# A fused convolution, attention and expert kernel: other fillers, a shorter group deviation, reordered output products

## The chip, the core and the metric

The kernel runs on one core of a Trainium2 chip. The metric is device time in microseconds (us), from one launch; several runs are made and their median is taken. The core has five engines that run side by side and meet at semaphores: TensorE (matrix products, into PSUM), VectorE, ScalarE, GpSimd and SyncE (which here issues the transfers).

## The reference

The input x has 4 images of 64 channels of 16 x 16 pixels. Three layers follow, each added to its input:

```python
x = x + involution(group_norm(x))          # 32 groups of 2 channels
t = tokens(x)                              # 4 x 256 tokens of 64
t = t + attention(layer_norm(t))           # 8 heads
t = t + experts(layer_norm(t))             # 8 experts, 2 used by an image
```

- group_norm: mean and variance over 2 channels and all pixels, `(g - m) / sqrt(s + eps)`.
- involution: from x a 1x1 convolution to 16 channels, batch norm with given statistics, relu, and a 1x1 convolution to 49 weights for each of 4 groups; each pixel is the sum of its 7 x 7 neighbours with these weights; then a 1x1 projection.
- attention: for each head, q^T k over all tokens gives a 64 x 64 matrix, which is normalised by its own mean and variance, put through a softmax, and applied to v; then the output projection Wo.
- experts: the mean over an image's tokens gives logits, a softmax, a scaling by expected load, a second softmax, and the two best experts; each is a gelu layer of 128 and a linear layer back, mixed by the gates; then a layer norm with gamma and beta.

## The kernel before

The program is written out engine by engine; every engine runs its own list in order, and waits for semaphores. Two images lie side by side in the 128 partitions (64 channels each), so there are two pairs of images, `t_` = 0 and 1, and four blocks of 128 tokens (`NQ` = 4). Nothing loops at run time.

Results of TensorE go to 8 PSUM banks. `CHUNKS` lists the results in the order in which they are made, with the engine that reads each; `SHARED` says which takes over the bank of another, and `homes` places the rest round the banks. `begin(name)` on TensorE waits until the earlier holder of the bank was read (`wait_read`), and returns the bank. An fp32 product takes two passes on TensorE, each a weight load and a matmul.

`keep_warm(name, n, cols)` issues `n` products of a tile of zeros, `cols` columns wide, whose results nobody uses; it calls `begin` first, also where `n` is 0. `WARM` holds the counts. "Filler" means such a product below.

The stages that matter here, in their order:

- Start. TensorE runs seven fillers, then one behind the arrival of `xg`, one behind the channel moments, one behind the root of the variance ("group_deviations"), and then the group product (`gn0`, `gn1`), which adds up the two channels of a group and spreads mean and scale. Its factors `gs` are made on VectorE (L675 to L685): the inverse deviation from ScalarE's root, and one correction step on it. The batch-norm scale is made in the same way in between, in `bn_t`. Then VectorE normalises (`normalise`, L697), TensorE multiplies with w1 (`y`), ScalarE applies scale, shift and relu (L530), and three "spread" products and the window transposes (L1003) follow.
- The involution's products, then the projection and the layer norm of tokens; the gram matrix of the tokens (`gram_part`, four of them, with fillers between), from it the heads' scores (`a..`), the row products (`rows`: 32 passes on `gm` and `wqc`), four transposes of `e` (L1154), and the variance of the scores from the row squares and the sums of squares `ast`.
- The softmax, then the value products `v00` to `v11`, read by VectorE as `pv` (L820 for the first half of the heads, L825 for the second), and the output products of pv and the centred Wo (`woc`), which add up in `m`: the heads in four steps `i`, in each the two partition halves `l` and the two pairs `t_`.
- `m` is copied to SBUF by VectorE and ScalarE; four products of `eT` and `m` add to the residual products in `o0` to `o3`; squares, roots and scales give `f`, which TensorE sums and transposes (`fsum`, `fT`, L1220) behind six fillers. `b2_products` is a small product, used much later; `restore` keeps o plus beta for the end, eight steps, of which the last stands late.
- Logits, softmax, choice (`pick`), which VectorE and GpSimd load into registers to copy the chosen weights (L342); the expert products; the squares of the result (`nq`), their roots, and the output.

## Time and profile before

| | |
|---|---|
| median of 3 runs | 54.08 us (53.98 to 54.11) |
| the profiled execution | 53.69 us |
| its span in the profile | 51.8 us |
| TensorE matmul busy | 42.9 us (83% of the span) |
| VectorE, ScalarE, GpSimd busy | 35.2, 31.6, 16.4 us |

The profile is one execution. Its span starts with the first instruction and ends with the last; some 1.9 us of the device time lie outside. Matmuls are pipelined, and their ends are modelled: two that overlap both count, so the starts say more than the busy time. All times in rows are us from the start of the span, durations in us unless marked ns.

### The profile page before, as it was taken

To read this page: it belongs to the slowest core of one execution; us is meant where nothing else is said; L and a number is where in the kernel's file an instruction comes from. 1 tells how busy PE (TensorE), PEld (TensorE's weight loads), DVE (VectorE), ACT (ScalarE), POOL (GpSimd) and SP (SyncE) were. 2 spreads that over 40 slices of the span, in tenths; PEclk is the share of its full clock that TensorE was granted. 3 is DMA by queue.
4 is the path that set the end of the run, shared out by engine and by line. 5 is a ranking of instruction groups with operands and counts; after the bars stand their busy time and mean duration, and the time that the engine had idled before them with its cause. 6 is when DMAs were issued, how large, how long until landed. Compare 5 with 4: busy or idle time off the path is not lost.

```text
span 51.8 us, 1844 instructions
## 1 busy us (share of the span) xinstructions
PE 42.9 (83%) x678; PEld 30.2 (58%) x678; DVE 35.2 (68%) x143; ACT 31.6 (61%) x92; POOL 16.4 (32%) x45
## 2 busy tenths in 40 slices
PE   0999989999998989799499588799976899999400
PEld 0331343799996966489367467584831367869300
DVE  3788996567997986460909269459968387983940
ACT  0363419969856794265339992279965967996200
POOL 5996009100038730983000000630000279332000
PEclk9999999999999999999999999999999999999985
DMA  0499888465000000000000006600000000000051
GB/s 0 129 326 286 218 234 223 114 89 173 8 0 13 0 0 0 6 13 0 0 6 0 0 13 133 272 0 0 13 0 0 0 0 0 6 0 0 0 150 53
DMA packets 3608, 3.21 MB, mean 62 GB/s; under 512 B 912, under 2 KB 2960, under 8 KB 3600
## 3 DMA queue, kind: packets, MB, share of 16 engines
q1 hardware_dynamic: 3072, 2.80, 19.5%
q10 hardware_dynamic: 432, 0.30, 2.0%
q8 instruction: 5, 0.08, 0.6%
q0 software_dynamic: 96, 0.00, 0.2%
q14 instruction: 3, 0.02, 0.1%
HBM read 2.84 MB, written 0.26 MB: 60 GB/s over the span
## 4 chain that ended last, share of the span: by engine, by line
PE 66%; DVE 13%; issue 7%; ACT 6%; DVEq 1%; ACTq 0%
PE ps L968 61%; PE ps L1003 3%; DVE res L955 3%; ACT L585 2%; DVE pv L825 1%; DVE pv L820 1%; PE ps L1220 1%; ACT prob L588 1%; PE ps L1154 1%; ACT yf L530 1%; DVE xp L697 1%; DVEq L335 1%; ACT rt L608 1%; DVE rsum L817 1%; DVE m L833 1%
## 5 line engine op out<-in xcount | busy, mean ns | idle before, releaser
L968 PE MATMUL ps<-zeros 128*128 128x512 bf16 (+1 forms) x38 | 11.6, 426 | 1.7 <-DVE zeros L664 1.2
L968 PEld LDWEIGHTS ps<-zeros 128*128 128x128 bf16 x38 | 3.4, 107 | 6.1 <-issue 1.4
L622 ACT ACTIVATE h<-ps,b1s 128x256 f32<-128x256 f32 x8 | 3.2, 473 | 0.8 <-PE ps L968 0.8
L319 DVE COPY wt<-ps 128x512 f32<-128x512 f32 x4 | 2.7, 688 | 1.3 <-PE ps L968 1.2
L342 POOL COPY w1s_g<-fw 128x128 f32 x4 | 1.2, 292 | 7.3 <-DVE pick L904 6.8
L968 PEld LDWEIGHTS ps<-yc,taps 128*128 128x128 bf16 x128 | 3.3, 96 | 0.3 <-issue 0.3
L968 PE MATMUL ps<-yc,taps 128*128 128x32 bf16 x128 | 3.4, 176 | 0.1
L450 POOL TENSOR_SCALAR w2m<-w2m 128x8 f32<-128x8 f32 x1 | 0.2, 245 | 9.0 <-DVE w2m L830 9.0
L482 ACT ACTIVATE wt<-ps 128x512 f32<-128x512 f32 x4 | 2.3, 596 | 0.7 <-PE ps L968 0.6
L479 ACT ACT_TABLE_LOAD x1 | 1.3, 1283 | 2.1 <-issue 2.1
L968 PE MATMUL ps<-fT,w1s 64*128 64x256 f32 x8 | 2.3, 403 | 0.2 <-DVE w1s L342 0.2
L1003 PE MATMUL ps<-consts,xp 128*128 128x128 f32 x16 | 2.4, 282 | 0.0
L482 ACT ACTIVATE xw<-ps 128x512 f32<-128x512 f32 x4 | 2.3, 592 | 0.0
L968 PE MATMUL ps<-fT,w1s_g 64*128 64x256 f32 x8 | 2.2, 398 | 0.0
L968 PE MATMUL ps<-wt,xw 128*32 128x64 f32 x128 | 2.2, 220 | 0.0
L368 POOL COPY taps<-w2c 128x140 bf16<-128x140 bf16 (+1 forms) x3 | 1.2, 493 | 3.1 <-DVE w2c L709 3.1
L805 DVE TENSOR_REDUCE ast<-asq 128x8 f32<-128x512 f32 x2 | 1.3, 680 | 1.2 <-ACT asq L576 1.2
L423 POOL TENSOR_SCALAR wkm<-wks 128x8 f32<-128x8 f32 x1 | 0.2, 243 | 5.7 <-DVE wks L732 5.7
L968 PE MATMUL ps<-h,w2s 128*64 128x256 f32 x16 | 2.1, 386 | 0.0
L968 PEld LDWEIGHTS ps<-wt,xw 128*32 128x32 f32 x128 | 1.9, 110 | 0.2
L407 POOL MEMSET taps<- 128x2240 bf16 x1 | 2.0, 1967 | 0.0
L864 DVE SCALAR_TENSOR_TENSOR t2b<-ps,betas 128x64 f32<-128x64 f32 x8 | 1.9, 274 | 0.0
(202 smaller groups left out, 120.0 us busy)
## 6 DMA issues: line engine op xcount, KB each, us to landing
fw<-in_fw SPq DMA_DIRECT2D x1, 512.0 KB, 3.6
wvT<-in_wvT SPq DMA_DIRECT2D x1, 260.0 KB, 3.6
x<-in_x SPq DMA_DIRECT2D x2, 128.0 KB, 3.9
wq<-in_L_attn_Wq SPq DMA_DIRECT2D x2, 128.0 KB, 3.1
wk<-in_L_attn_Wk SPq DMA_DIRECT2D x2, 128.0 KB, 3.4
fw<-in_fw SPq DMA_DIRECT2D x1, 256.0 KB, 3.8
out<-res SPq DMA_DIRECT2D x4, 64.0 KB, 1.6
xg<-in_x ACTq DMA_DIRECT2D x1, 128.0 KB, 2.8
```

The source lines that it names most:

```text
L319: copy(wt[:, :, :, :, :, g, w0:w0 + 8].rearrange("p l t q r w -> p (l t q) r w"), src.rearrange("p (w r q) -> p q r w", w=8, r=2)).then_in ...
L342: eng.tensor_copy(dst[:, b // 2, k, :].unsqueeze(1), fw1[:, bass.ds(expert, 1), :]).then_inc(copied, 1)
L368: copy(dst, w2c[:, :, :, lo:hi]).then_inc(done, 1)
L407: return pool.memset(ap, 0.0).then_inc(const[name], 1)
L479: act.preload_act_table(ACT.Sqrt)
L482: return act.activation(dst, src, ACT.Copy)
L622: act.activation(h[:, b, k, :], bank(f"h{TOPK * t_ + k}{l}")[:, 0:HW], ACT.Gelu, bias=b1s[:, b, k:k + 1]).then_inc(read_a, 1)
L805: dve.reduce_sum(ast[:, i, :, :], asq[:, i, :, :, :], AX.X).then_inc(made["score_sums"], 1)
L864: ins = dve.scalar_tensor_tensor(t2b[:, j, :], tokens(f"o{i}")[:, l, :], bank(f"o{i}")[:, l * (TC - 1):l * (TC - 1) + 1], betas[:, l, :], ...
L955: ins = dve.scalar_tensor_tensor(res[:, j, :], bank(f"u{i}")[:, (j - 2 * i) * C:(j - 2 * i + 1) * C], nrs[:, j:j + 1], t2b[:, j, :], ALU.m ...
L968: return pe.matmul(dst, lhsT, rhs, start=start, stop=stop)
L1003: ins = pe.transpose(dst[:, j * P:(j + 1) * P], xp[:, t_, 2 * q:2 * q + WINR, :], ident)
```

## The change

- Start: twelve short fillers (64 columns, 32 rows of the result) are put in after the seven long ones, ahead of the wait for `xg`. VectorE makes the reciprocal of the variance while ScalarE takes the root, and the scale is then root times that reciprocal plus the reciprocal of the root, in one step, without the correction (the signs and the factor in the `group` matrix change with it). The batch-norm scale is made in the same form, and two steps of ScalarE change places.
- The single fillers of 512 columns around the gram parts become four of 128 columns; one filler more behind the logits and one more behind the loads.
- `pv` of the first half of the heads is made in two steps, as that of the second half. The output products wait for each step, alternate between the halves `l` inside the pairs `t_`, and have no `keep_warm` of zero fillers between. `m` takes the bank that `o3` had, and `o3` that of `v00`; the residual product of `o3` moves behind the products of `m`.
- `b2_products` moves behind the four products with `m`, its read on VectorE behind the last normalisation.
- The last `restore` moves ahead of the register loads of the choice.
- Half of the second pair's squares is made on VectorE.

```diff
-WARM = {"start": 7, "stats": 2, "bands": 1, "norm1": 1, "gram": 1, "last": 4, "scores": 2, 
-        "values": 0, "m": 2, "output": 6, "norm2": 0,
-        "logits": 2, "choice": 3, "loads": 4}
+WARM = {"start": 7, "short": 12, "stats": 2, "norm1": 4, "last": 4, "gram": 4, "scores": 2,
+        "output": 6, "logits": 3, "choice": 3, "loads": 5}
...
-    ("o1", "O"), ("o2", "O"), ("o3", "O"), ("m", "V"),
+    ("o1", "O"), ("o2", "O"), ("m", "V"), ("o3", "O"),
...
-SHARED = {"gm0": "d3", "gm1": "gram", "m": "v00", "fsum": "v00", ...
+SHARED = {"gm0": "d3", "gm1": "gram", "o3": "v00", "fsum": "m", ...
...
+            act.wait_ge(dma["w2"], 16)
+            copy(w2a[:, :], w2r[:, :]).then_inc(made["w2_first"], 1)
             act.wait_ge(dma["front"], 16)
             act.activation(bn_t[:, 0:1], bnv[:, 3:4], ACT.Sqrt, bias=eps[:, :]).then_inc(made["bn_std"], 1)
-            act.wait_ge(dma["w2"], 16)
-            copy(w2a[:, :], w2r[:, :]).then_inc(made["w2_first"], 1)
...
-            act.activation(nq[:, 1, :], sums[:, 1, :], ACT.Square).then_inc(made["squared_by_scalar"], 1)
+            act.activation(nq[:, 1, TOK:], sums[:, 1, TOK:], ACT.Square).then_inc(made["squared_by_scalar"], 1)
...
-            dve.tensor_scalar(gs[:, 0:1], gmv[:, 0:1], -2.0, None, ALU.mult).then_inc(made["group_scales"], 1)
+            dve.tensor_scalar(gs[:, 0:1], gmv[:, 0:1], 2.0, None, ALU.mult).then_inc(made["group_scales"], 1)
+            after_mark()
+            mark(dve.reciprocal(gd[:, 3:4], gd[:, 1:2]))
             dve.wait_ge(dma["front"], 16)
             mark(dve.tensor_scalar(bn_t[:, 1:2], bnv[:, 3:4], EPS, None, ALU.add))
             dve.wait_ge(made["group_deviations"], 1)
-            link(dve.reciprocal(gd[:, 2:3], gd[:, 0:1]))
-            mark(dve.scalar_tensor_tensor(gd[:, 3:4], gd[:, 2:3], gd[:, 2:3], gd[:, 1:2], ALU.mult, ALU.mult))
+            mark(dve.reciprocal(gd[:, 2:3], gd[:, 0:1]))
+            dve.wait_ge(v_seq, steps[0] - 1)
+            mark(dve.reciprocal(bn_t[:, 3:4], bn_t[:, 1:2]))
+            dve.wait_ge(v_seq, steps[0] - 1)
+            dve.scalar_tensor_tensor(gs[:, 1:2], gd[:, 0:1], gd[:, 3:4], gd[:, 2:3], ALU.mult, ALU.add).then_inc(made["group_scales"], 1)
+            dve.wait_ge(made["w2_first"], 1)
+            dve.scalar_tensor_tensor(w2d[:, :], w2a[:, :], mask[:, 0:1], w2r[:, :], ALU.mult, ALU.add).then_inc(made["w2_rest"], 1)
             dve.wait_ge(made["bn_std"], 1)
             mark(dve.reciprocal(bn_t[:, 2:3], bn_t[:, 0:1]))
-            dve.wait_ge(v_seq, steps[0] - 1)
-            dve.scalar_tensor_tensor(gs[:, 1:2], gd[:, 3:4], -3.0, gd[:, 2:3], ALU.add, ALU.mult).then_inc(made["group_scales"], 1)
-            after_mark()
-            mark(dve.scalar_tensor_tensor(bn_t[:, 3:4], bn_t[:, 2:3], bn_t[:, 2:3], bn_t[:, 1:2], ALU.mult, ALU.mult))
-            dve.wait_ge(made["w2_first"], 1)
-            dve.scalar_tensor_tensor(w2d[:, :], w2a[:, :], mask[:, 0:1], w2r[:, :], ALU.mult, ALU.add).then_inc(made["w2_rest"], 1)
-            after_mark()
-            mark(dve.scalar_tensor_tensor(bn_t[:, 4:5], bn_t[:, 3:4], -3.0, bn_t[:, 2:3], ALU.add, ALU.mult))
...
             normalise(0)
             after_mark()
-            mark(dve.tensor_scalar(bn_t[:, 6:7], bnv[:, 0:1], bn_t[:, 4:5], -0.5, ALU.mult, ALU.mult))
+            mark(dve.scalar_tensor_tensor(bn_t[:, 4:5], bn_t[:, 0:1], bn_t[:, 3:4], bn_t[:, 2:3], ALU.mult, ALU.add))
             normalise(1)
             after_mark()
+            link(dve.tensor_scalar(bn_t[:, 6:7], bnv[:, 0:1], bn_t[:, 4:5], 0.5, ALU.mult, ALU.mult))
...
-                if i == 0:
-                    dve.tensor_tensor(pv[:, i, :, :, :, :].rearrange("p l k t c -> p l (k t) c"), src[:, :, :, 0:C],
-                                      rsum[:, i, :, :].unsqueeze(3).to_broadcast([P, 2, HH, C]), ALU.mult).then_inc(read_v, 2)
-                else:
...
+                for k in range(2):
+                    two_ = slice(2 * k, 2 * k + 2)
+                    ins = dve.tensor_tensor(pv[:, i, :, k, :, :], src[:, :, two_, 0:C], rsum[:, i, :, two_].unsqueeze(3).to_broadcast([P, 2, 2, C]), ALU.mult)
+                    if k == 0:
+                        ins.then_inc(made["values_weighted"], 1)
+                ins.then_inc(read_v, 2)
...
-            dve.wait_ge(made["b2_products"], 1)
-            dve.tensor_copy(b2c[:, :], bank("loads")[:, B2COL:B2COL + EXP]).then_inc(made["b2_centred"], 1)
             output_stats(1)
...
             normalise_output(3)
+            dve.wait_ge(made["b2_products"], 1)
+            dve.tensor_copy(b2c[:, :], bank("loads")[:, B2COL:B2COL + EXP]).then_inc(made["b2_centred"], 1)
...
+            restore(7)
             dve.wait_ge(made["choice"], 1)
...
             dve.scalar_tensor_tensor(gdiag[:, :], sign_of, rs[:, 6:7], offs_of, ALU.mult, ALU.add).then_inc(made["gate_rows"], 1)
-            restore(7)
...
             mixed_columns(1)
+            dve.wait_ge(made["ffn_columns"], NQ - 1)
+            dve.tensor_tensor(nq[:, 1, 0:TOK], sums[:, 1, 0:TOK], sums[:, 1, 0:TOK], ALU.mult).then_inc(made["squared_by_vector"], 1)
...
-            def keep_warm(name, n, cols=BANK):
+            def keep_warm(name, n, cols=BANK, rows=P):
...
-                    mm(dst[:, 0:cols], zeros[:, 0:P], zeros[:, 0:cols])
+                    mm(dst[0:rows, 0:cols], zeros[:, 0:rows], zeros[:, 0:cols])
...
             keep_warm("gn0", WARM["start"])
+            keep_warm("gn0", WARM["short"], C, QUAD)
             pe.wait_ge(dma["xg"], 16)
...
-            keep_warm("a00", WARM["norm1"])
+            keep_warm("a00", WARM["norm1"], P)
...
+            dst = begin("m")[:, M0:]
             for i in range(HH):
                 if i % 2 == 0:
-                    if i == 0:
-                        residual(NQ - 1)
-                        dst = begin("m")[:, M0:]
-                    else:
-                        keep_warm("logits", WARM["values"])
-                if i == 2:
-                    pe.wait_ge(made["values_weighted"], 1)
-                elif i % 2 == 0 or i == 3:
+                    pe.wait_ge(made["values_weighted"], i // 2 + 1)
+                else:
                     wait_read(pe, f"v{i // 2}1")
-                for l in range(2):
-                    for t_ in range(BH):
+                for t_ in range(BH):
+                    for l in range(2):
...
-            pe.wait_ge(dma["fb2"], 16)
-            mm(begin("loads")[:, B2COL:B2COL + EXP], cen[:, 1:1 + P], b2T[:, :]).then_inc(made["b2_products"], 1)
+            residual(NQ - 1)
...
+            pe.wait_ge(dma["fb2"], 16)
+            mm(begin("loads")[:, B2COL:B2COL + EXP], cen[:, 1:1 + P], b2T[:, :]).then_inc(made["b2_products"], 1)
             keep_warm("logits", WARM["output"])
```

## Rows read from the trace of the kernel before

**Rows 1.** The page's chain that ended last, shares by engine.

```profile
PE 66%; DVE 13%; issue 7%; ACT 6%; DVEq 1%; ACTq 0%
```

**Rows 2.** Timeline, start: start, duration, engine, line, what, count, [idle before <-releaser].

```profile
1.21 4.49 PE L968 MATMUL ps<-zeros 128*128 128x512 bf16 x10 [1.21 <-DVE zeros L664]
...
5.04 0.16 DVE L680 RECIPROCAL gd<-gd 128x1 f32<-128x1 f32 x1
...
5.24 0.22 DVE L681 SCALAR_TENSOR_TENSOR gd<-gd 128x1 f32<-128x1 f32 x1
...
5.49 0.16 DVE L685 SCALAR_TENSOR_TENSOR gs<-gd 128x1 f32<-128x1 f32 x1
...
5.80 0.39 PE L968 MATMUL ps<-gs,front 64*128 64x2 f32 x4
...
7.25 0.16 DVE L706 TENSOR_TENSOR bn_t<-front,bn_t 128x1 f32<-128x1 f32 x1
...
7.65 0.46 ACT L530 ACTIVATE yf<-ps,bn_t 128x128 f32<-128x128 f32 x1 [1.13 <-PE ps L968]
```

**Rows 3.** Timeline, two groups of later fillers.

```profile
20.27 0.28 PE L968 MATMUL ps<-zeros 128*128 128x64 bf16 x4
...
34.44 1.46 PE L968 MATMUL ps<-zeros 128*128 128x512 bf16 x6
```

**Rows 4.** Row products: chain, timeline, stretches by engine, DMA from 22 to 26.

```profile
24.67 0.68 issue
```

```profile
24.00 0.58 PEld L968 LDWEIGHTS ps<-gm,wqc 64*64 64x64 f32 x30
```

```profile
core 0: us, PE busy (x) PEld busy (x) DVE busy (x) ACT busy (x) POOL busy (x), PEclk, DMA share, GB/s
18.86:25.34 6.48, 5.12 (x122) 4.24 (x121) 3.63 (x13) 3.32 (x15) 2.72 (x5) 1.00 0.01 4
25.34:33.43 8.09, 6.67 (x122) 5.26 (x122) 4.73 (x12) 5.10 (x9) 0.64 (x2) 1.00 0.23 68
```

```profile
GB/s 0 0 0 0 0 0 0 0 0 0 164 0 0 0 0 0 0 0 0 0 0 0 0 0 0 0 0 0 0 0 0 0 0 0 0 0 0 0 0 0
...
q8 instruction: 1, 0.02, 1.4%
```

**Rows 5.** Timeline, from the score squares to their sum.

```profile
23.84 1.09 ACT L576 ACTIVATE asq<-ps 128x512 f32<-128x512 f32 x2 [0.52 <-PE ps L968]
...
24.47 1.28 DVE L805 TENSOR_REDUCE ast<-asq 128x8 f32<-128x512 f32 x2 [1.23 <-ACT asq L576]
...
26.38 0.30 PEld L968 LDWEIGHTS ps<-ast,consts 128*128 128x128 f32 x2
```

**Rows 6.** Timeline, pv, the output products and m.

```profile
30.36 0.69 DVE L820 TENSOR_TENSOR pv<-ps,rsum 128x512 f32<-128x512 f32 x1
...
31.17 0.59 PEld L968 LDWEIGHTS ps<-woc,pv 128*64 128x64 f32 x16 [0.45 <-DVE pv L820]
...
31.20 0.76 DVE L825 TENSOR_TENSOR pv<-ps,rsum 128x256 f32<-128x256 f32 x2
...
32.01 0.60 PEld L968 LDWEIGHTS ps<-woc,pv 128*64 128x64 f32 x16 [0.25 <-DVE pv L825]
...
32.85 0.28 DVE L833 COPY m<-ps 64x130 f32<-64x130 f32 x1 [0.31 <-PE ps L968]
...
33.44 0.97 PEld L968 LDWEIGHTS ps<-m,eT 128*128 128x128 f32 x8 [0.47 <-issue]
```

**Rows 7.** Timeline, the first two blocks of normalised output.

```profile
35.28 0.26 DVE L858 TENSOR_TENSOR f<-ps,fsd 128x128 f32<-128x128 f32 x1
...
35.67 0.51 ACT L603 ACTIVATE f<-ps,fsd 128x64 f32<-128x64 f32 x2
```

**Rows 8.** Timeline, the choice and the end.

```profile
38.54 0.09 PEld L968 LDWEIGHTS ps<-rt,rs 4*4 4x4 f32 x2 [0.77 <-DVE rs L893]
...
40.09 0.33 PEld L968 LDWEIGHTS ps<-zeros 128*128 128x128 bf16 x3 [0.89 <-DVE pick L904]
...
40.77 0.23 DVE L342 COPY w1s<-fw 128x128 f32 x1 [0.56 <-issue]
...
47.66 0.18 DVE L951 RECIPROCAL nrs<-nsd 128x4 f32<-128x4 f32 x1 [0.80 <-ACT nsd L627]
```

**Rows 9.** Busy time of the engines between 7.2 and 10 us, columns as above.

```profile
7.20:10.00 2.80, 2.71 (x44) 1.82 (x44) 2.05 (x7) 2.28 (x7) 1.44 (x5) 1.00 0.78 208
```

More of the change, by code:

```diff
@@ L102 @@
 INDEX = {name: j for j, (name, _) in enumerate(CHUNKS)}
-SHARED = {"gm0": "d3", "gm1": "gram", "m": "v00", "fsum": "v00", "fT": "v01", "logits": "v10", "loads": "v11", "gates": "o2", "q0": "o3",
+SHARED = {"gm0": "d3", "gm1": "gram", "o3": "v00", "fsum": "m", "fT": "v01", "logits": "v10", "loads": "v11", "gates": "o2", "q0": "o3",
           "h00": "loads", "h10": "fT", "h01": "fsum", "h11": "logits", "h20": "o0", "h21": "o1", "h30": "h00", "h31": "h10",
@@ L288, in build @@
         made = {k: sem("done_" + k) for k in (
-            "taps", "e", "b2_products", "f_squares", "wos", "wo_mean", "wo_centred", "residual_read", "wqs", "wks", "wqm", "wkm", "wqc", "wkc", "prob", "f", "gate", "w1s", "w1s_g", "w2s", "w2s_g", "b1s", "b1s_g", "w2_means", "w2_centred", "b2_centred", "bias_columns", "bias_columns_g", "bias_scaled", "bias_sums", "gamma_of", "squared_by_pool", "squared_by_scalar", "ffn_columns", "ffn", "w2c_g", "bn_std", "e_g", "e_nb", "attn_in", "f_g",
+            "taps", "e", "b2_products", "f_squares", "wos", "wo_mean", "wo_centred", "residual_read", "wqs", "wks", "wqm", "wkm", "wqc", "wkc", "prob", "f", "gate", "w1s", "w1s_g", "w2s", "w2s_g", "b1s", "b1s_g", "w2_means", "w2_centred", "b2_centred", "bias_columns", "bias_columns_g", "bias_scaled", "bias_sums", "gamma_of", "squared_by_pool", "squared_by_scalar", "squared_by_vector", "ffn_columns", "ffn", "w2c_g", "bn_std", "e_g", "e_nb", "attn_in", "f_g",
             "e_rs", "f_rs", "f_nb", "attn_out", "e_var", "e_std", "f_var", "f_std", "n_std", "n_rs", "result",
@@ L818, in _ @@
                 dve.wait_ge(made["row_sums_inverted"], i + 1)
-                if i == 0:
-                    dve.tensor_tensor(pv[:, i, :, :, :, :].rearrange("p l k t c -> p l (k t) c"), src[:, :, :, 0:C],
-                                      rsum[:, i, :, :].unsqueeze(3).to_broadcast([P, 2, HH, C]), ALU.mult).then_inc(read_v, 2)
-                else:
-                    for k in range(2):
-                        two_ = slice(2 * k, 2 * k + 2)
-                        ins = dve.tensor_tensor(pv[:, i, :, k, :, :], src[:, :, two_, 0:C], rsum[:, i, :, two_].unsqueeze(3).to_broadcast([P, 2, 2, C]), ALU.mult)
-                        if k == 0:
-                            ins.then_inc(made["values_weighted"], 1)
-                    ins.then_inc(read_v, 2)
+                for k in range(2):
[4 more added lines that the diff above has]
+                ins.then_inc(read_v, 2)
             dve.wait_ge(dma["w_second"], 16)
@@ L1107, in _ @@
             gram_part(0, dst)
-            keep_warm("a00", WARM["norm1"])
+            keep_warm("a00", WARM["norm1"], P)
             gram_part(1, dst)
-            keep_warm("a00", WARM["norm1"])
+            keep_warm("a00", WARM["norm1"], P)
             gram_part(2, dst)
@@ L1113, in _ @@
             gram_part(3, dst).then_inc(written, 1)
-            keep_warm("a00", WARM["gram"])
+            keep_warm("a00", WARM["gram"], P)
             pe.wait_ge(dma["wq"], 32)
@@ L1284, in squares_of @@
                         pe.wait_ge(made["squared_by_pool"], s + 1)
+                    else:
+                        pe.wait_ge(made["squared_by_scalar" if s else "squared_by_vector"], 1)
                     ins = mm(dst[:, 2 * s:2 * s + 2], nq[:, t_, s * TOK:(s + 1) * TOK], half_of[:, 0:2])
@@ L1291, in _ @@
             squares_of(0)
-            pe.wait_ge(made["squared_by_scalar"], 1)
             squares_of(1)
@@ L1339, in front_layout @@
     p = np.arange(P)
-    f[:, F_GROUP:F_GROUP + P] = (p[:, None] % C == (p // C * GRP + p % C // 2)[None, :]) * -0.5
+    f[:, F_GROUP:F_GROUP + P] = (p[:, None] % C == (p // C * GRP + p % C // 2)[None, :]) * 0.5
     wpg = np.zeros((2, C, 2, C), np.float32)
```

## The prediction

> **What bounds the kernel now.** I read the shares of the chain of work that ended last first: TensorE holds 66% of the span, VectorE 13%, "issue" 7% [rows 1]. Almost every stage is a relay through TensorE with short steps of VectorE or ScalarE between, so what counts is when each handover comes, not how busy an engine is. Then I read the timeline stage by stage at the edited places [rows 2, 5 to 8], and last the "issue" pieces of the chain, times in which TensorE waits for nothing that the profile shows. The reader should see one of 0.68 us: the 32 row products ("rows", two instructions each, a weight load and a matmul) run at some 20 ns each, the thirtieth is issued before 24.7, and the last two start at 25.35, though they wait for no semaphore [rows 4]. No data can explain a pause inside a uniform group. A smaller pause stands at 33.44: the product with m starts 0.30 us after VectorE's copy of m ended (32.85 + 0.28), where the handover after pv took 0.12 (31.05 to 31.17) [rows 6]. Between the two pauses TensorE issues 122 matmuls and 122 weight loads, and between 18.86 and the first pause 122 and 121 [rows 4]: the pauses come at even distances in its instruction stream. In the 4 us before the first pause ends, the only DMA packet is one of the instruction queue, at 23.0 us [rows 4]. I read the pauses as TensorE reaching instructions that are not there yet. The Trainium skill (Runtime: NRT & Kernel Launch, "Instruction fetch mechanics") says that engines refill instructions in blocks of 256, and that crossing a block is mostly hidden; the distance agrees, the "hidden" does not, with 0.68 us on the chain.
>
> **The start: fillers and group deviation.** Before, the scales of the group product come out of three linked VectorE steps: reciprocal 5.04, product 5.24, last step 5.49 to 5.65, and TensorE starts at 5.80 [rows 2]. After, the reciprocal of the variance is made while ScalarE takes the root, and after the root only the reciprocal (5.04) and one step that reads another column as its scalar remain; such a step took 0.22 at 5.24. Ready at 5.46, so 0.19 sooner. But TensorE is not free then. Seven fillers at 0.43 each (ten took 4.49 [rows 2], half the pace of the later ones at 0.216 [rows 3]: 512 columns at the 1.2 and the 2.4 GHz level, though the granted-clock column prints full speed) end at 4.20. The twelve short ones have 64 columns; four such took 0.28 with 0.193 for the last, so 0.029 apart at the high level [rows 3], 0.058 at the low one: 0.70 for twelve, TensorE free at 4.90. Before them only the data of xg was awaited; after them come three long fillers in a row, 1.28 at the low level, 6.18 in all. Before, the clock had risen by the filler after the group product; if it rises as then, the last of the three is short and the group product starts at about 5.95. I take 5.95: 0.15 late. Bounds: 0.029 each and a risen clock, 5.60 (0.19 early, the VectorE gain in full), and 6.2 (0.40 late). In the batch-norm scale, one more step stands behind the second normalise: bn scale and shift end 0.19 after 7.41 (7.25 + 0.16) relative to the normalise, against a ScalarE start at 7.65 [rows 2], which costs 0.03. ScalarE's swapped copy and root are off this path. Sum of the start: +0.18.
>
> **Fillers around the gram products** become four of 128 columns instead of one of 512: the same columns, 0.21 us each time. Bounds: four at the 0.029 of the short ones, a gain of 0.1, and 0.06 more for a weight load that can't be done ahead; the gram parts wait for scaled tokens anyway, so I take nothing. One filler more behind "logits" and one behind "loads" (0.216 each) end inside the 0.77 and 0.89 us for which TensorE waits there [rows 8]; nothing, and 0.2 each if that cover were gone.
>
> **What the fillers do to the pauses.** Twelve short fillers and nine extra ones around the gram are 21, so 42 instructions more ahead of the row products. If the pause is tied to a position in the stream, it comes 42 instructions earlier in the program: after the ninth row product. The request for the missing block would be earlier by as many instructions as well, and those lie in the sparse stretch between 19.7 and 23 us, so it is earlier by one to two microseconds, more than the 0.68 that were missing. Then the row products end near 24.8 rather than 25.6. The next to end last is VectorE's second sum of squares, 24.47 + 1.28 = 25.75; TensorE's product with it is at 26.38 now and could start at 25.80 [rows 5]. That is -0.57 (bounds: 0, the pause stays on the path; -0.7). ScalarE's squares of the row products would begin when its previous work ends, 23.84 + 1.09 = 24.93 [rows 5], and are in time. The small pause moves in the same way from the product with m into the product that makes m, behind its second head pair, where TensorE waits for pv anyway: -0.18 (bounds 0 and -0.2).
>
> **The m product.** Before, pv of the first half is one step of 0.69, of the second half two of 0.76 together; now both are split: +0.07 on VectorE. TensorE's products come in two batches of sixteen passes, at 31.17 and 32.01, each about 0.5 us long at 0.030 per pass [rows 6]. The second batch should have begun when the first part of pv's second half was ready, at about 31.6; it began after all of it (31.20 + 0.76 = 31.96), because the zero-filler call on "logits" still waits for the bank's reader. The change drops that call: only eight passes remain behind pv, so -0.27 + 0.06 = -0.21 (bounds 0 and -0.3). Alternating halves: one pass of 130 columns on the full array takes 0.111 ((0.97 - 0.19) / 7) [rows 6], so 65 columns alone should take 0.055, but the passes come 0.030 apart: the halves already overlap in the old order. So nothing. The Trainium skill (TensorE: Matmul & The Clock Gate, "Part 3: Packing small matmuls") would have alternation win, since matmuls start strictly in order and only different column groups run together; by it the eight last passes would take 0.2 us less, and the row speaks against it. The fourth residual product moves behind the m product, into the 0.4 us in which TensorE waits for m; hidden.
>
> **Behind the output products.** The b2 product (two passes, 0.11 each) leaves a hidden place for one ahead of six fillers that end at 34.44 + 6 x 0.216 = 35.73, already after the first normalised output (35.28 + 0.26) [rows 3, 7]: +0.22 there; but the second pair waits for ScalarE until 36.18 (35.67 + 0.51) [rows 7], and soaks up half. Its read now stands on VectorE ahead of the restores, and so ahead of the step that makes the token sums: about +0.1 as well, at the same time. Together +0.10 (bounds 0 and +0.25).
>
> **Choice.** The last restore now stands ahead of the register loads: one more dispatch before the weight copy at 40.77 [rows 8]: +0.05 (bounds 0, and 0.2 if the loads wait for it to finish).
>
> **The end.** Half of a squaring goes from ScalarE to an idle VectorE (0.80 us idle at 47.66 [rows 8]). The second roots come sooner, but VectorE takes them up only after its four result steps: nothing.
>
> **Sum.** +0.18 - 0.57 - 0.18 - 0.21 + 0.10 + 0.05 = -0.63. The profiled execution took 53.69 (span 51.8 and 1.9 around it) and would take 53.06; it lies 0.39 below the median of the runs, and the same difference makes 54.08 - 0.63 = 53.45.
>
> **Rivals.** (1) The pause stays on the path, its place moved but no shorter. For it: I have only two pauses, and the request rule is inferred. Then without -0.57: 54.0, and 54.2 if the small one stays too. (2) The block arrives at a fixed moment, not at a fixed distance: the pause begins after the ninth row product, still ends at 25.35, and 23 products of 0.02 follow where 2 did, +0.42 in place of -0.57: 54.45, slower. It decides as soon as the block comes after 24.9. Against it: the packet at 23.0 follows no event of another queue that I can see. (3) The twelve narrow fillers delay the rise of the clock: the stretch from the group product to the window transposes then runs at the low level. TensorE is busy 2.71 us of 7.2 to 10.0 [rows 9], and a 512-column filler takes twice as long from start to start at the low level; if a third to a half of that busy time is streaming, 0.9 to 1.3 is added: 54.3 to 54.8. It decides from 0.63 on. Against it: the array stays as busy as before in time. (4) The start costs nothing and the other terms reach their good ends: 53.0.
>
> **Chances.** Forecast 0.47 (53.15 to 53.75), rival 4 0.13, rival 1 0.25, rival 2 0.07, rival 3 0.08. Rivals 2 and 3 are slower, rival 1 is spread over no change (0.15), slower (0.07) and a little faster (0.03). So faster 0.63, within 0.3% (0.16 us, about what a measurement of this kernel tells from nothing) 0.15, slower 0.22. The range for 8 in 10 reaches from 53.0 to 54.3.
>
> **What would show it.** Row products without a gap, the product with the sums of squares some 0.5 us earlier against the gram products; the group product near 5.95, with TensorE and not VectorE before it; the last m passes in a batch of eight; the 0.30 handover at m down to 0.12. A first batch of passes closer than 0.030 would show that alternating matters. A pause of over 0.3 us at another place on the chain, or long fillers at 0.43 after 6.2 us, would make the prediction wrong.

## The result, and the profile after

The changed kernel takes 55.28 us (median of 4 runs, 54.98 to 56.15), the kernel before 54.03 us (4 runs, 53.65 to 54.11) beside it. The ratio is 1.023, 95% interval 1.016 to 1.030: slower, where 53.45 us had been forecast. Some executions are slower as a whole at a lower granted clock, the run of 56.15 us among them (0.963, the other three 0.978 to 0.980); the ratios in this document leave such runs out. The profiled execution took 55.31 us with a span of 53.1; before it was 53.69 with 51.8, so the traces can be laid side by side.

The page of the changed kernel, the chain's shares by engine (before: [rows 1]):

```profile
PE 66%; DVE 15%; issue 8%; ACT 5%; DVEq 1%; ACTq 0%
```

"Issue" should have shrunk with the pause, and grew. The chain of the changed kernel in order of time (start, us, what) shows why:

```profile
17.03 1.35 PE ps L965 x32
18.39 0.84 issue
19.23 2.60 PE ps L965 x24
...
25.00 1.27 PE ps L965 x71
26.27 0.71 issue
26.98 0.52 PE ps L965 x23
```

There are two pauses. The second is that of [rows 4], which was to vanish. The first is new, and costs more. The timeline of the changed kernel says what stands around both:

```profile
17.75 0.64 PE L965 MATMUL ps<-wt,xw 128*32 128x64 f32 x28
...
19.23 0.31 PE L965 MATMUL ps<-wt,xw 128*32 128x64 f32 x4 [0.84 <-issue]
19.23 0.14 PEld L965 LDWEIGHTS ps<-wt,xw 128*32 128x32 f32 x3 [1.00 <-issue]
...
25.93 0.25 PEld L965 LDWEIGHTS ps<-gm,wqc 64*64 64x64 f32 x9
...
26.41 1.28 DVE L804 TENSOR_REDUCE ast<-asq 128x8 f32<-128x512 f32 x2 [1.23 <-ACT asq L575]
26.98 0.44 PEld L965 LDWEIGHTS ps<-gm,wqc 64*64 64x64 f32 x23 [0.80 <-issue]
...
28.28 0.30 PEld L965 LDWEIGHTS ps<-ast,consts 128*128 128x128 f32 x2
```

The row products are cut after the ninth of 32, exactly the place forecast. But the pause is as long as before (0.71 against 0.68 on the chain), and the product with ast follows 0.59 us after ast's end (27.69 and 28.28), where it was 0.63 before (25.75 and 26.38 [rows 5]). And the 32 products of wt and xw are cut after the 28th, with 1.00 us without a weight load. Between the pauses the counts are the same as before, in the changed kernel's stretches:

```profile
core 0: us, PE busy (x) PEld busy (x) DVE busy (x) ACT busy (x) POOL busy (x), PEclk, DMA share, GB/s
...
19.22:26.97 7.75, 6.38 (x121) 5.54 (x120) 4.06 (x15) 4.45 (x20) 3.02 (x6) 1.00 0.01 3
26.97:33.57 6.60, 5.46 (x123) 4.31 (x123) 3.81 (x11) 4.83 (x8) 0.00 (x0) 1.00 0.09 9
```

That is some 121 pairs, as from 18.86 to 25.34 in [rows 4]. So the new pause is the boundary that stood at 18.86 in the kernel before, where TensorE lost little. If the records of semaphore instructions are counted too, the two cuts come after the 705th and the 961st recorded TensorE instruction, 256 apart, and the cut of the kernel before comes after its 961st. The Trainium skill (Runtime: NRT & Kernel Launch, "Instruction fetch mechanics") gives blocks of 256 instructions; here the trace agrees.

The start, timeline of the changed kernel (before: [rows 2]):

```profile
1.21 5.32 PE L965 MATMUL ps<-zeros 128*128 128x512 bf16 x22 [1.21 <-DVE zeros L663]
...
4.31 0.89 PEld L965 LDWEIGHTS ps<-zeros 128*32 128x32 bf16 x14 [0.83 <-issue]
...
5.10 0.16 DVE L681 RECIPROCAL gd<-gd 128x1 f32<-128x1 f32 x1
...
5.30 0.22 DVE L685 SCALAR_TENSOR_TENSOR gs<-gd 128x1 f32<-128x1 f32 x1
...
6.46 0.48 PE L965 MATMUL ps<-gs,front 64*128 64x2 f32 x4
...
8.48 0.46 ACT L529 ACTIVATE yf<-ps,bn_t 128x128 f32<-128x128 f32 x1 [2.23 <-DVE bn_t L705]
```

VectorE has the scales at 5.52 (5.30 + 0.22; 5.65 before), but the fillers hold TensorE until 6.46 (5.80 before). And ScalarE's yf now waits for VectorE's last step on the batch-norm shift (bn_t, L705), where it waited for TensorE before. The output products, timeline of the changed kernel (before: [rows 6]), and the copy of the chosen weights (before: [rows 8]):

```profile
33.09 0.76 DVE L820 TENSOR_TENSOR pv<-ps,rsum 128x256 f32<-128x256 f32 x2
33.57 0.65 PEld L965 LDWEIGHTS ps<-woc,pv 128*64 128x64 f32 x16 [0.26 <-DVE pv L820]
...
34.47 0.28 DVE L828 COPY m<-ps 64x130 f32<-64x130 f32 x1
...
34.85 0.97 PEld L965 LDWEIGHTS ps<-m,eT 128*128 128x128 f32 x8 [0.27 <-issue]
```

```profile
42.23 0.23 DVE L341 COPY w1s<-fw 128x128 f32 x1 [0.36 <-issue]
```

To see where time went, I cut each span at starts that all kernels share. Each column is the difference of two such starts in one profiled execution. The columns: first group product; from it to the first product of yc and taps; to VectorE's copy of gram; to ScalarE's root asd; to the end of the last pv; to VectorE's copy of m; to the first product with m and eT; to the end.

| kernel | group | yc | gram | asd | pv | m | m,eT | end | span |
|---|---|---|---|---|---|---|---|---|---|
| before | 5.80 | 4.41 | 10.94 | 5.72 | 5.09 | 0.89 | 0.59 | 18.31 | 51.75 |
| changed | 6.46 | 4.63 | 11.99 | 5.69 | 5.08 | 0.62 | 0.41 | 18.26 | 53.14 |
| e1_no_short | 5.84 | 4.52 | 10.94 | 5.84 | 5.08 | 0.85 | 0.41 | 18.25 | 51.73 |
| e2_short_only | 6.46 | 4.59 | 11.68 | 5.43 | 5.09 | 0.89 | 0.41 | 18.20 | 52.75 |
| e3_recut | 5.85 | 4.41 | 11.98 | 5.43 | 5.08 | 0.90 | 0.41 | 18.29 | 52.35 |
| e4_m_only | 5.91 | 4.41 | 10.95 | 5.72 | 5.08 | 0.63 | 0.66 | 18.13 | 51.49 |
| f1_two_wide | 6.21 | 4.55 | 10.94 | 5.59 | 5.08 | 0.62 | 0.41 | 18.25 | 51.65 |
| f2_row_block | 5.80 | 4.60 | 10.94 | 5.14 | 5.09 | 0.90 | 0.41 | 18.19 | 51.07 |
| f3_all_but_fillers | 5.69 | 4.74 | 11.16 | 5.62 | 5.08 | 0.62 | 0.41 | 18.25 | 51.57 |
| f7_row_block_m | 5.92 | 4.41 | 10.94 | 5.14 | 5.09 | 0.62 | 0.41 | 18.19 | 50.72 |
| f4_full_rows | 6.23 | 4.74 | 12.06 | 5.54 | 5.08 | 0.62 | 0.41 | 18.24 | 52.92 |
| f5_six_short | 6.09 | 4.53 | 11.89 | 5.90 | 5.08 | 0.62 | 0.41 | 18.25 | 52.77 |
| f6_m_in_turn | 5.79 | 4.56 | 10.94 | 5.71 | 5.76 | 0.64 | 0.41 | 18.22 | 52.03 |
| g1_start_one_step | 5.72 | 4.52 | 11.15 | 5.61 | 5.08 | 0.63 | 0.41 | 18.20 | 51.32 |

Changed against before: +0.66 and +0.22 at the start, +1.05 up to gram, -0.03 and -0.01, then -0.27 and -0.18 at the output products, -0.05 at the end: +1.39. The loss has two parts, and only the second was in the sum at all.

### The profile page after: what moved, and what is told of

It reads as the page before. It is cut to its first block, busy times and chain, and to the rows that moved or that the text cites. A ratio compares the mean times of both kernels' runs of the same rounds, so it can differ in the third digit from the quotient of the medians.

```text
span 53.1 us, 1890 instructions
## 1 busy us (share of the span) xinstructions
PE 44.0 (83%) x701; PEld 31.2 (59%) x701; DVE 35.5 (67%) x145; ACT 31.6 (59%) x92; POOL 16.3 (31%) x45
## 4 chain that ended last, share of the span: by engine, by line
PE 66%; DVE 15%; issue 8%; ACT 5%; DVEq 1%; ACTq 0%
PE ps L965 61%; PE ps L1001 3%; DVE res L952 3%; ACT L584 2%; DVE pv L820 2%; PE ps L1214 1%; ACT prob L587 1%; PE ps L1152 1%; DVE w2c L708 1%; DVE xp L695 1%; ACT rt L607 1%; DVE rsum L816 1%; DVE gram L796 1%; DVE nrs L948 1%; DVE zeros L663 1%
## 5 line engine op out<-in xcount | busy, mean ns | idle before, releaser
L965 PE MATMUL ps<-zeros 128*128 128x512 bf16 (+3 forms) x61 | 12.9, 350 | 1.5 <-DVE zeros L663 1.2
L965 PEld LDWEIGHTS ps<-zeros 128*128 128x128 bf16 (+1 forms) x61 | 4.9, 111 | 6.0 <-issue 2.5
L547 ACT ACTIVATE dsb_first<-ps,consts 128x128 f32<-128x128 f32 x4 | 1.5, 367 | 1.6 <-PE ps L965 1.5
L774 DVE SCALAR_TENSOR_TENSOR dsb<-ps,consts,dsb_first 128x128 f32<-128x128 f32 x4 | 1.4, 344 | 1.3 <-ACT dsb_first L547 1.3
L437 POOL TENSOR_TENSOR e<-ts,e_sd 128x512 f32<-128x512 f32 x1 | 1.0, 1042 | 3.1 <-DVE ts L769 3.1
```

The costliest lines, as they stand in the source:

```text
L547: act.activation(dsb_first[:, i, :].rearrange("p (h w) -> p h w", h=8), product_of(i, 0), ACT.Copy, scale=own[:, 0:1]).then_inc(made["firs ...
L774: dve.scalar_tensor_tensor(dsb[:, i, :].rearrange("p (h w) -> p h w", h=8), product_of(i, 1), own[:, 1:2], dsb_first[:, i, :].rearrange("p ...
L965: return pe.matmul(dst, lhsT, rhs, start=start, stop=stop)
```

## The experiments

**The changed kernel without the twelve fillers.**

```diff
             keep_warm("gn0", WARM["start"])
-            keep_warm("gn0", WARM["short"], C, QUAD)
```

> The changed kernel without its twelve short fillers, 24 TensorE instructions fewer at the start; all else of the change stays. Theory A (the fillers delay the group product, and their 24 instructions move the end of a 256-instruction block into the products of wt and xw, where the next block isn't there yet): the group product starts near 5.65 instead of 6.46, no pause in the products of wt and xw (it was 0.84 us at 18.39), a pause of some 0.7 us stays in the row products, about 20 of the 32 before it; the attention stage keeps its gain of 0.4 us. Time 53.4 to 54.0. Theory B (the later rise of TensorE's clock is the loss, wherever the instructions lie): the start comes back by 0.9 us, the pause of 0.84 stays, about 54.4 to 54.7. Theory C (the loss is in the other edits): over 54.8.

Measured: 53.77 us, ratio 0.9985 (0.9938 to 1.0032). Without them the loss against the kernel before is gone: group product at 5.84, and the stage up to gram takes 10.94 as before. The nine extra instruction pairs around gram move the cut in the row products to after the 21st, and the pause there stays (asd stage 5.84). The gain of 0.4 expected at the output products is only half there: the stage of m takes 0.85, not 0.62 as in the changed kernel. Its timeline says why:

```profile
31.94 0.88 PEld L965 LDWEIGHTS ps<-woc,pv 128*64 128x64 f32 x16 [0.26 <-DVE pv L820]
```

The same sixteen weight loads take 0.65 in the changed kernel. Here the next boundary lies inside the last eight of them, and TensorE starts nothing from 32.44 to 32.63.

**Only the twelve fillers, on the kernel before**, and **the same 24 instructions without more time**: the start's seven long fillers become five long ones and fourteen short ones.

```diff
-            keep_warm("gn0", WARM["start"])
+            keep_warm("gn0", 5)
+            keep_warm("gn0", 14, C, QUAD)
```

> The kernel before with nothing but the twelve short fillers. Theory A: group product 0.8 us later (6.4 to 6.6 instead of 5.80), a new pause of 0.8 us in the products of wt and xw, the pause of the row products after about 18 of 32 instead of 30; in all 1.6 to 2.0 us slower, 55.6 to 56.0. Theory B: 0.9 us slower, 54.9. Theory C: within 0.3 of 54.03.

> The kernel before with five long and fourteen short fillers at the start in place of seven long: as many columns and about as much time, but 24 TensorE instructions more, as many as the change adds there. Theory A: group product and clock as before (within 0.2), but the pause of 0.8 us in the products of wt and xw appears: 54.8 to 55.2. Theory B: if the narrow fillers delay the clock by themselves, the group product starts on time and the stretch behind it is slower by 0.2 to 0.4, no new pause: 54.2 to 54.5. Theory C: 54.0.

Measured: the fillers alone 54.73 us, ratio 1.016 (1.006 to 1.027); the recut 54.72 us, ratio 1.020 (1.010 to 1.030). For the first, 55.6 to 56.0 had been expected: both losses came (+0.84 by the first product of yc, +0.74 in the stage up to gram), but smaller than thought, and the later stages gave back 0.6, half of it because the pause in the row products shortened. The second run decides: its start is no later (5.85), no other edit is in it, and the stage up to gram takes 11.98 instead of 10.94. Its timeline:

```profile
16.91 0.64 PE L968 MATMUL ps<-wt,xw 128*32 128x64 f32 x28
18.39 0.31 PE L968 MATMUL ps<-wt,xw 128*32 128x64 f32 x4 [0.84 <-issue]
18.39 0.14 PEld L968 LDWEIGHTS ps<-wt,xw 128*32 128x32 f32 x3 [1.00 <-issue]
...
25.25 0.42 PEld L968 LDWEIGHTS ps<-gm,wqc 64*64 64x64 f32 x18
...
25.99 0.32 PEld L968 LDWEIGHTS ps<-gm,wqc 64*64 64x64 f32 x14 [0.32 <-issue]
```

Same cut after the 28th product, same 0.84 and 1.00. The row products are cut after 18 = 30 - 12, and here the pause did shorten, to 0.32.

**Only the output products' edits, on the kernel before** (weighted values by halves, both halves of the partitions in turn, m and o3 swap banks, last residual behind), and the same **without the alternation**:

```diff
-                for t_ in range(BH):
-                    for l in range(2):
+                for l in range(2):
+                    for t_ in range(BH):
```

> The kernel before with only the middle part of the change: pv in halves, the output products alternating and without the zero-count filler call, m and o3 in exchanged banks, the last residual product behind m. Theory A: the start and the pause in the row products stay as they are, the four products with m start 0.4 us sooner after the values: 0.3 to 0.5 us faster, 53.55 to 53.75. If alternating halves gives something of its own, the passes of a batch are closer than 0.030 us and it is more than 0.6. Theory C (this part costs time): slower than 54.03.

> The kernel before with the edits of the output products, but with the products not alternating between the two halves of the partitions: four of each half in turn, as the kernel before has them. If the alternation is worth anything, the last batch of m takes longer than in the kernel with alternation (0.03 us per pass there); if only the earlier start counts (values by halves, banks swapped, residual moved), the stage takes the same time within 0.03 us, and the copy of m comes as early after the last pv.

Measured: 53.83 us (4 runs: 53.19, 53.42, 54.23 and 54.24, too far apart for a ratio) and, one execution, 53.96 us. What this part is worth is therefore read from the stages alone. The stage from pv to the copy of m takes 0.63 and 0.64: the alternation is worth nothing that shows. The last sixteen weight loads take the same 0.65 (the last eight of them wait for pv; from the first matmul of these eight to the last it is 0.23 with alternation, 0.24 without), timelines of the kernel with alternation and of that without:

```profile
31.79 0.65 PEld L964 LDWEIGHTS ps<-woc,pv 128*64 128x64 f32 x16 [0.26 <-DVE pv L821]
```

```profile
32.48 0.65 PEld L964 LDWEIGHTS ps<-woc,pv 128*64 128x64 f32 x16 [0.25 <-DVE pv L821]
```

(The second's longer time up to pv, 5.76, lies in a stretch of that one execution in which the granted clock was 0.50, from 28 to 31 us; at the output products it was 1.00 again. The first's 0.66 ahead of the product with m and eT is the small pause, still at its old place. The second, with as many instructions ahead, takes 0.41 there.)

**The changed kernel with the same 768 columns in two fillers**, 4 instructions instead of 24:

```diff
-            keep_warm("gn0", WARM["short"], C, QUAD)
+            keep_warm("gn0", 1)
+            keep_warm("gn0", 1, BANK // 2)
```

> The changed kernel with its twelve short fillers replaced by two wide ones, of 512 and of 256 columns, which stream the same 768 columns in 4 TensorE instructions instead of 24. Theory A (what costs is the place of the 256-instruction boundary, and beside it the time that the fillers take at the start): the boundary number 705 goes back behind the products of wt and xw, as in the changed kernel without fillers; the start still ends late, group product at about 6.3 to 6.5 us, but the pause of 1.00 us within those products is gone. The later stages then stand some 0.9 us ahead of the changed kernel: 54.3 to 54.5 us, ratio to the kernel before 1.005 to 1.01. Theory B (only the occupied start costs, through the later product and the later rise of the clock): as the changed kernel, 55.3 us, ratio 1.02. Theory C (the other edits cost): also 1.02, with the pause of 1.00 us still there.

Measured: 53.47 us, ratio 0.993 (0.989 to 0.998). The same columns at the same place, and by the ratios the kernel is 3% faster than as changed, faster even than the one before. Its 32 products of wt and xw run uncut:

```profile
17.36 0.49 PEld L965 LDWEIGHTS ps<-wt,xw 128*32 128x32 f32 x32
17.36 0.65 PE L965 MATMUL ps<-wt,xw 128*32 128x64 f32 x32
```

I had expected 54.3 to 54.5 and so a smaller gain; the stage up to gram gives back 1.05 and the start another 0.33. Against the changed kernel's span it is 1.49 less, of which 1.05 is the pause.

**The row products' boundary moved by three pairs**, on the kernel before, four fillers of 64 columns as one of 256:

```diff
-            keep_warm("a00", WARM["last"], C)
+            keep_warm("a00", 1, 4 * C)
```

> The kernel before with one edit: the four fillers of 64 columns behind the third product of ts and t become one of 256 columns, the same columns in 6 TensorE instructions fewer. Theory A (the pause sits at instruction 961, whatever stands there): in the kernel before this is after 30 of the 32 row products; 3 passes further on it lies behind the last of them, among the transposes of e, where TensorE has half a microsecond to wait for ScalarE's squares anyway. The last row product then comes near 24.8 us instead of 25.43, and asd 0.3 to 0.5 us earlier than 26.87: ratio 0.990 to 0.995, about 53.6 us. Rival (the pause belongs to the row products, for example to their operands): nothing changes, the pause of 0.68 us stays ahead of the 31st, ratio 1.000.

Measured: 53.03 us, ratio 0.992 (0.989 to 0.995), from one line. Its timeline:

```profile
24.19 0.59 PEld L968 LDWEIGHTS ps<-gm,wqc 64*64 64x64 f32 x32
...
25.00 0.38 ACT L582 ACTIVATE rsq<-ps 64x16 f32<-64x16 f32 x2
25.16 0.60 PE L1154 MATMUL ps<-consts,e 128*128 128x128 f32 x4 [0.30 <-issue]
25.17 0.36 PEld L1154 LDWEIGHTS ps<-consts,e 128*128 128x128 f32 x3 [0.24 <-issue]
```

The row products are whole; the pause sits behind the weight load of the first transpose of e, while ScalarE squares the row products. The asd stage takes 5.14 instead of 5.72.

**Half the fillers**, and **all twelve at the full array width** (one execution each):

```diff
-            keep_warm("gn0", WARM["short"], C, QUAD)
+            keep_warm("gn0", 6, C, QUAD)
```

```diff
-            keep_warm("gn0", WARM["short"], C, QUAD)
+            keep_warm("gn0", WARM["short"], C)
```

> The changed kernel with 6 short fillers instead of 12. Theory A: start earlier by 6 x 0.053 = 0.32 us (group product near 6.1), and boundary 705 comes 12 instructions later in the work, behind the last product of wt and xw, among the products of cen and x. The missing block is there no sooner relative to these products (about 3.1 us after the first of them), so that part of the pause stays: 0.5 to 0.8 us, at a new place, ahead of a product of cen and x or of wpc and dsb. If instead the pause belonged to the products of wt and xw, it would stay ahead of one of them or vanish.

> The changed kernel with its twelve short fillers written with all 128 weight columns, so to all 128 output partitions, instead of a quarter of them: the same 64 columns streamed each and the same number of instructions. If the gaps of 0.12 to 0.14 us ahead of the first short filler and ahead of the long filler behind them come from the change of tile shape, they go and the group product stands near 6.2 us instead of 6.46; if the fillers' number and columns alone set it, it stays at 6.4 to 6.5. In both cases the pause at boundary 705 within the products of wt and xw stays, 0.9 to 1.0 us.

Measured: 54.75 and 55.06 us in the one execution. With six fillers the cut lies among the products of cen and x, as expected, and its weight load comes 0.59 late; the row products are cut after the 15th = 9 + 6. A pause of the products themselves is ruled out. Timeline of the kernel with six:

```profile
18.23 0.41 PEld L965 LDWEIGHTS ps<-cen,x 128*128 128x128 f32 x3
19.23 0.19 PEld L965 LDWEIGHTS ps<-cen,x 128*128 128x128 f32 x1 [0.59 <-issue]
```

At full width the fillers follow the long ones without a gap, weight loads of that kernel:

```profile
4.17 0.79 PEld L965 LDWEIGHTS ps<-zeros 128*128 128x128 bf16 x13 [0.28 <-issue]
...
6.23 0.51 PEld L965 LDWEIGHTS ps<-gs,front 64*128 64x128 f32 x4 [0.84 <-issue]
```

The first short filler starts at 4.17 and not 4.31, and the group product at 6.23 and not 6.46: by this one execution, two changes of tile width cost 0.23. The pause among the products of wt and xw stays, as expected (stage up to gram 12.06).

**Everything but the fillers, with the boundaries moved; row boundary and output products; and that with the one-step deviation.** The first is the changed kernel without the twelve fillers and with one wide filler at each place of the gram stage; the second adds the edits of the output products to the moved boundary, on the kernel before; the third adds to this the start of VectorE and ScalarE from the change.

> The changed kernel without the twelve short fillers, with the fillers of the gram stage as in the kernel before (one of 512 columns each, not four of 128) and the four of 64 as one of 256: all edits of the other engines and of the output products stay. By theory A both boundaries, 705 and 961, lie at places where TensorE waits anyway: no pause in the products of wt and xw or in the row products. Start 0.1 to 0.2 us earlier by the one-step deviation, rows end 0.4 us earlier, output products another 0.3 to 0.45: 53.0 to 53.3 us, ratio 0.98 to 0.987. If the boundary has no part in it, the ratio is that of the changed kernel without short fillers, 0.9985, or at best 0.992 for the output products alone.

> The kernel before with the fillers of 64 columns as one of 256 and the edits of the output products (weighted values by halves, alternating halves of the partitions, banks of m and o3 swapped, last residual moved behind). It is the sum of two experiments: the row boundary (theory A: -0.3 to -0.5 us) and the output products (-0.15 to -0.3 us measured by the stages of the kernel that had them alone). Together 53.2 to 53.5 us, ratio 0.985 to 0.992. If the boundary does nothing: 0.995 to 0.998. Against the run with all other edits it tells what VectorE's shorter start and the edits at the end are worth: 0.1 to 0.2 us if the one-step deviation counts, nothing if it does not.

> The kernel with the output products' edits and the one filler of 256 columns, and in addition only the start part of the change: group deviation in one step on VectorE, with the order of ScalarE's and VectorE's instructions behind it. If the one-step deviation counts (two steps of VectorE fewer ahead of the group product, 1.20 us from the aggregate to the group product instead of 1.40 us in the kernels that had it and had not), the group product comes at 5.60 to 5.72 us instead of 5.80 to 5.92, and every later stage stands 0.1 to 0.2 us earlier: ratio 0.983 to 0.986, about 52.6 us. Rival: the third long filler ends no earlier, or the later order of the batch-norm scale (yf waits for VectorE) eats it: ratio 0.9875 as without it, or above.

Measured: 53.03 us, ratio 0.989 (0.985 to 0.993); 52.72 us, 0.988 (0.983 to 0.992); 52.95 us, 0.986 (0.981 to 0.990). The three can't be told from one another; each beats both kernels. For the first, 0.98 to 0.987 had been expected: a little too much. The one-step deviation shows in the timelines, without and with it:

```profile
4.53 0.21 DVE L673 BATCH_NORM_AGGREGATE gmv<-gst 128x2 f32<-128x12 f32 x1
...
5.92 0.39 PE L964 MATMUL ps<-gs,front 64*128 64x2 f32 x4 [0.35 <-DVE gs L685]
```

```profile
4.52 0.21 DVE L673 BATCH_NORM_AGGREGATE gmv<-gst 128x2 f32<-128x12 f32 x1
...
5.72 0.39 PE L964 MATMUL ps<-gs,front 64*128 64x2 f32 x4
```

From aggregate to group product 1.20 instead of 1.39: the 0.19 forecast, where no filler stands in the way. The kernel's time does not show it (ratio 0.986 against 0.988). In the profiled execution with it, 0.11 of it went in the next stage (4.52 instead of 4.41), where ScalarE's yf now waits for VectorE. Two longer pauses cost the rest and more, though the instructions of TensorE are the same in both kernels: 0.21 up to gram, from a boundary that lies further ahead, among the first products of wt and xw, and 0.47 in the asd stage, where the pause is 0.85 on the chain. Timeline and chain of the kernel with the one-step deviation:

```profile
7.62 0.46 ACT L530 ACTIVATE yf<-ps,bn_t 128x128 f32<-128x128 f32 x1 [1.31 <-DVE bn_t L706]
...
14.99 1.22 PEld L964 LDWEIGHTS ps<-wt,xw 128*32 128x32 f32 x81 [0.28 <-issue]
```

```profile
24.91 0.85 issue
```

The pause of 0.85 stands in the first kernel of the three as well (asd stage 5.62). In both the block's packet starts 1.8 to 1.9 us after the copy of gram, in the second kernel and in that with the row boundary alone 1.5. So a boundary moved behind the row products is worth 0.6 us in two profiled executions and 0.1 in two others.

## Why the prediction was wrong

**Place of the pauses: right, and incomplete.** "If the pause is tied to a position in the stream, it comes 42 instructions earlier in the program: after the ninth row product" came out to the pass, and in eight kernels the count of pairs ahead gives the cut: 30, 9, 21, 18, 18, 19, 9 and 15. But the same count was not made for the boundary ahead of it, at 18.86, which stands in [rows 4] as the end of a stretch of 121 pairs. Twenty-four instructions shift it from behind the products of wt and xw to after the 28th of the last 32, where TensorE stops for a microsecond. This is +1.05 that no term and no rival holds. The recut (no time added, ratio 1.020) and the two wide fillers (time added, ratio 0.993) show it from both sides.

**The failed step** is the next sentence: "The request for the missing block would be earlier by as many instructions as well". Its term was -0.57 and measured -0.03. The page lists each block's transfer as one packet of the instruction queue; from 23 to 27 us in the changed kernel:

```profile
GB/s 0 0 0 0 0 0 0 0 0 0 0 0 0 0 164 0 0 0 0 0 0 0 0 0 0 0 0 0 0 0 0 0 0 0 0 0 0 0 0 0
...
q8 instruction: 1, 0.02, 1.6%
```

It begins near 24.4 (the fifteenth of forty slices), 1.4 us after the copy of gram at 23.08; before, it began at 23.0, 1.9 after the copy at 21.15. So it came half a microsecond sooner in the program, not one to two, and the cut came 21 pairs sooner. What I had called sparse did not matter: what matters is when the block arrives against when TensorE gets there. In 23 pauses of the 14 traces TensorE goes on 1.3 to 1.6 us after the packet's end, whatever it was doing (the small pause is another matter, see below). With the cut after the 9th product the pause ended 3.90 us after the copy of gram instead of 4.20, and 23 products follow instead of 2. In time that is rival 1 (the term is nothing); in mechanism it lies between rivals 1 and 2, since the block came earlier, but by less than the cut did. The value -0.57 itself can be reached: in the two kernels in which the cut lies behind the row products and the block comes early, the stage is shorter by 0.58 (5.72 to 5.14). What sends the request stays open; the packet starts 1.93, 1.77 and 1.53 us after the copy of gram in the three kernels whose instructions up to there are the same, and 1.28 to 1.39 after it in those with the cut among the products of wt and xw, where the earlier pause comes in between.

**The start: mis-sized.** Forecast 5.95 for the group product, bound 6.2, measured 6.46; by the first product of yc it is +0.88 where +0.18 stood. The twelve fillers took what was computed (0.89 for fourteen weight loads; 0.053 apart), but each change of tile width cost another 0.12, 0.23 in all, and the third long filler still ran at the low level of the clock, where the prediction had it short. Behind the group product another 0.22 was lost. Half of it is the change's own: in the changed kernel without the twelve fillers, whose four group passes take 0.39 as before, this stage takes 4.52 instead of 4.41. The steps on the batch norm stand there, and +0.03 had been taken for them; ScalarE's yf is released by VectorE's bn_t in all seven kernels with the new start and by TensorE in all seven with the old one, and starts 1.90 to 1.93 after the group product where the passes take 0.39, against 1.85 to 1.88. The other half is the pace of the group passes (0.48 in the changed kernel), and that differs between executions: in the kernel with only the row boundary moved, whose start is that of before, they take 0.59 from 5.80, against 0.39 from 5.80 in [rows 2], and this stage 4.60. Rival 3, a clock held low through the windows, did not happen: the two fillers behind the group product run at the high level in the changed kernel, 0.60 for two. VectorE's earlier scales were right (5.52 against 5.46), and the 0.19 shows at the group product once TensorE is free, though not in the time of the kernel.

**The small pause: right in size, not in what it was.** From the copy of m to the product with it 0.41 instead of 0.59: the -0.18. It moved with the count, as the 0.19 us of the kernel without the short fillers also says. But in the kernel before, this block's packet had ended at 31.11, 2.3 us before TensorE went on at 33.44, so it was not the same wait as the large one, and one kernel with the same count of instructions ahead of it shows no such pause (0.41). What it is made of stays open. **The m product: right, slightly larger.** 0.89 to 0.62 is -0.27 where -0.21 stood, and the batch of eight is there. The alternation is worth nothing, as [rows 6] had said: both orders take 0.65 for sixteen. The Trainium skill (TensorE: Matmul & The Clock Gate, "Part 3: Packing small matmuls") has matmuls in different tiles of the array run together and start strictly in order, from which alternation should have won; the traces here do not bear it out.

**Behind the output products, choice, end: too dear.** +0.15 was forecast and about -0.05 measured over the whole stretch. The b2 product costs 0.05: from the product with m and eT to the first step on the logits all six kernels with its new place take 4.34, and six of the eight with the old one 4.29 to 4.30 (the other two, with the small pause, 4.32 and 4.22). The last restore and the extra fillers cost nothing that shows: from that product to the copy of the chosen weights it is 7.35 in the changed kernel and 7.33 before. The gram fillers of 128 columns cost nothing by themselves (stage up to gram 10.94 without the short ones); they only moved the cuts behind them.

**Sum.** In the forecast's order: +0.88 for +0.18, -0.03 for -0.57, -0.18 for -0.18, -0.27 for -0.21, -0.05 for +0.15, and +1.05 for the boundary that was not followed. It adds up to +1.40, the difference of the spans but for rounding. The two that make the forecast wrong are the -0.57 that did not come and the +1.05 that was in no term.

## What to carry to other kernels

Fillers that keep the clock up are also instructions: fill time with few wide ones. Where TensorE issues small matmuls in dense runs, find the pauses that wait for nothing, count the instructions between them, and after any edit ahead of them follow every boundary, those that now cost nothing first. Moving one out of a dense run by three pairs gave 0.8% here with one line. The gain depends on when the block arrives, and that differs by up to 0.4 us between executions of the same instructions.

## What the runs showed of the hardware that had not been expected

- A boundary between two blocks of 256 TensorE instructions held TensorE up for 0.2 to 1.0 us where a dense run of small products crosses it, and for less than 0.1 us on the chain where it stood at 18.86 in the kernel before. The Trainium skill (Runtime: NRT & Kernel Launch, "Instruction fetch mechanics") calls the crossing mostly hidden; the traces here disagree for such runs.
- TensorE resumes 1.3 to 1.6 us after the block's packet has ended (23 pauses in 14 traces, with packets of 0.88 to 1.41 us). Two small pauses, ahead of the product with m and eT, ended 2.0 and 2.3 us after theirs.
- A change of the weight's width between fillers cost about 0.12 us at the low level of the clock (0.23 for two).
- The moment at which the clock rises differs between executions with the same start: the group passes took 0.39 and 0.59 us.
